# A factorization machine on one core: the first half's input loads go in pairs

## What is computed

```python
x_reg = input_data @ W_lin.T + b_lin
emb = input_data @ factors
sum_squared = jnp.square(emb.sum(axis=1))
squared_sum = (jnp.square(input_data) @ jnp.square(factors)).sum(axis=1)
h = jax.nn.relu(emb @ W1.T + b1)
h = jax.nn.relu(h @ W2.T + b2)
dnn_out = h @ W3.T + b3
x = x_reg + 0.5 * (sum_squared - squared_sum)[:, None] + dnn_out
x = 0.5 + jax.nn.sigmoid(x) * 5.0
```

## Time and profile before

| | us |
|---|---|
| median of 3 runs | 135.52 |
| lowest, highest | 135.15, 135.66 |
| the profiled execution | 135.22 |
| its span, first to last instruction | 133.0 |
| TensorE busy | 104.9 (79%) |
| VectorE busy | 53.3 (40%) |
| ScalarE busy | 64.1 (48%) |
| DMA, mean over the span | 393 GB/s |

### The profile page before, as it was taken

How to read it: one execution, slowest core, us unless ns; L and a number is a source line. 1 busy time by engine, 2 the same in 40 slices (tenths; PEclk the granted TensorE clock), 3 DMA queues, 4 the chain that set the end, 5 groups by cost and what they waited for, 6 DMA issues and landing times.

```text
span 133.0 us, 2839 instructions
## 1 busy us (share of the span) xinstructions
PE 104.9 (79%) x1113; PEld 31.9 (24%) x1113; DVE 53.3 (40%) x51; ACT 64.1 (48%) x72; POOL 13.7 (10%) x48
## 2 busy tenths in 40 slices
PE   6088976939978778877878869996966966989992
PEld 6022211102211111111212312211111111345871
DVE  0391550423522531531540291550451451576571
ACT  4030752625724733733744294752652662465851
POOL 3017011010410110011011001152000000000000
PEclk9999999995999999999999999999999999999999
DMA  4999999999999999999999999999999999999700
GB/s 121 404 398 424 424 438 419 434 414 434 429 429 429 424 434 419 434 429 429 429 434 424 424 429 424 434 429 429 414 438 419 428 442 418 401 416 411 296 14 1
DMA packets 4592, 52.25 MB, mean 393 GB/s; under 512 B 530, under 2 KB 662, under 8 KB 1642
## 3 DMA queue, kind: packets, MB, share of 16 engines
q1 hardware_dynamic: 4586, 52.16, 93.4%
HBM read 52.16 MB, written 0.00 MB: 392 GB/s over the span
## 4 chain that ended last, share of the span: by engine, by line
DMA 62%; PE 29%; ACT 3%; SPq 3%; issue 2%; DVE 1%; ACTq 0%
DMA xr<-in_x_groups 51%; PE p_lin L460 23%; DMA xr<-in_x_end 11%; ACT sq L292 2%; PE p_sq L460 2%; PE p_h L543 2%; SPq L230 1%; PE p_tot L460 1%; PE p_h L574 1%; PE p_tot L556 0%; DVE h L412 0%; DVE h L407 0%; SPq L228 0%; SPq L227 0%; PE p_tot L563 0%
## 5 line engine op out<-in xcount | busy, mean ns | idle before, releaser
L292 ACT ACTIVATE sq<-xr 128x1536 f32<-128x1536 f32 (+1 forms) x40 | 48.5, 1262 | 47.7 <-DMA xr<-in_x_groups 47.7
L387 DVE TENSOR_TENSOR sq<-xr 128x1536 f32<-128x1536 f32 x20 | 35.1, 1759 | 57.0 <-DMA xr<-in_x_groups 56.9
L460 PE MATMUL p_lin<-xr,wr 128*17 128x512 f32 x320 | 38.9, 604 | 16.0 <-DMA xr<-in_x_groups 16.0
L460 PE MATMUL p_lin<-sq,wz 128*18 128x512 f32 x320 | 39.3, 608 | 2.3 <-ACT sq L292 1.0
L460 PEld LDWEIGHTS p_lin<-xr,wr 128*17 128x17 f32 x320 | 8.0, 97 | 45.0 <-issue 24.4
L460 PEld LDWEIGHTS p_lin<-sq,wz 128*18 128x18 f32 x320 | 8.4, 99 | 33.0 <-ACT sq L292 18.7
L267 POOL COPY wr<-hd x20 | 8.4, 422 | 70.9 <-PE p_lin L460 70.4
L395 DVE TENSOR_TENSOR sq<-xr 128x320 f32<-128x320 f32 (+5 forms) x15 | 10.4, 724 | 8.1 <-DMA xr<-in_x_end 8.1
L301 ACT ACTIVATE sq<-xr 128x320 f32<-128x320 f32 (+5 forms) x15 | 9.1, 652 | 7.1 <-DMA xr<-in_x_end 7.1
L460 PE MATMUL p_lin<-xr,hd 128*17 128x352 f32 (+1 forms) x128 | 10.0, 380 | 1.5 <-DMA xr<-in_x_end 1.5
L460 PE MATMUL p_lin<-sq,ws 128*18 128x352 f32 x64 | 6.6, 459 | 0.0
(11 more groups left out here) (50 smaller groups left out, 35.7 us busy)
## 6 DMA issues: line engine op xcount, KB each, us to landing
xr<-in_x_groups SPq DMA_DIRECT2D x20, 2048.0 KB, 15.4
xr<-in_x_end SPq DMA_DIRECT2D x1, 2112.0 KB, 10.8
xr<-in_x_end SPq DMA_DIRECT2D x3, 640.0 KB, 12.3
xr<-in_x_end SPq DMA_DIRECT2D x1, 1760.0 KB, 14.6
xr<-in_x_end SPq DMA_DIRECT2D x1, 1056.0 KB, 12.6
hd<-in_head SPq DMA_DIRECT2D x1, 935.0 KB, 4.8
xr<-in_x_end SPq DMA_DIRECT2D x1, 704.0 KB, 14.0
xf<-in_x_first SPq DMA_DIRECT2D x1, 512.0 KB, 5.8
```

Of the source, the lines that this page charges most:

```text
L292: nc.scalar.activation(sq[:, s, c:c + n, :], xr[:, s, c:c + n, :], ACT.Square).then_inc(act_squared, 1)
L387: nc.vector.tensor_tensor(sq[:, s, 0:BY_DVE, :], xr[:, s, 0:BY_DVE, :], xr[:, s, 0:BY_DVE, :], ALU.mult).then_inc(dve_squared, 1)
L460: return nc.tensor.matmul(out, lhsT, rhs, start=False, stop=False, skip_group_check=True)
```

## The change

The host puts groups 0 and 1, 2 and 3, and so on of the first half side by side, so that one partition's row of a pair is 32 KB of memory without a gap (`x_pairs`). One DMA brings such a pair into two neighbouring slots and counts on the even slot's semaphore. The first half so has 6 DMAs of 4 MB in place of 12 of 2 MB. The second half and `x_end` keep their sizes.

In the first half TensorE multiplies both groups of a pair and then adds the squares of both. The first squares' matmul of each group, issued when the group is multiplied and all of its squares are made, increments a new semaphore, `x_used`; SP waits for that one in the first half, for both groups of a pair, and no longer for `sq_used`. From the first group of the second half on, SP waits for `sq_used` as it did.

TensorE in the first half's loop before: two groups, one after the other. Rows named `xr,wr` multiply, rows named `sq,wz` add squares.

The diff's core:

```diff
+TWO = 2
+PAIR_PITCH = TWO * CHUNKS * HALF + 64
...
+        def landed(engine, r, s, h):
+            if h == 0:
+                engine.wait_ge(x_landed[s - s % TWO], 16 * (r + 1))
+            elif s % TWO == 0:
+                engine.wait_ge(x_landed[s], 16 * (r + 1))
+            else:
+                engine.wait_ge(x_landed[s], 16 * (r + (1 - ROUNDS[0])))
...
-            for s in range(RING):
-                sp.dma_start(xr[:, s].rearrange("p c b -> p (c b)"), x_groups[s, :, 0:CHUNKS * HALF]).then_inc(x_landed[s], 16)
+            for t in range(RING // TWO):
+                sp.dma_start(xr[:, TWO * t:TWO * t + TWO].rearrange("p s c b -> p (s c b)"),
+                             x_pairs[t, :, 0:TWO * CHUNKS * HALF]).then_inc(x_landed[TWO * t], 16)
-            with sp.Fori(1, sum(ROUNDS)) as r:
+            with sp.Fori(1, ROUNDS[0]) as r:
+                for t in range(RING // TWO):
+                    sp.wait_ge(x_used, RING * r + (TWO * t + TWO - RING))
+                    sp.dma_start(xr[:, TWO * t:TWO * t + TWO].rearrange("p s c b -> p (s c b)"),
+                                 x_pairs[bass.ds(RING // TWO * r + t, 1), :, 0:TWO * CHUNKS * HALF]
+                                 .rearrange("g p n -> (g p) n")).then_inc(x_landed[TWO * t], 16)
+            with sp.Fori(ROUNDS[0], sum(ROUNDS)) as r:
...
-                pe.wait_ge(act_squared, len(BY_ACT) * g + 1)
+                pe.wait_ge(act_squared, len(BY_ACT) * g + (2 if h == 0 else 1))
                 for c in range(BY_DVE + BY_ACT[0]):
-                    add_mm(quad(p_lin[h], c, WZ, 0, HALF), wz[:, s, c, :], sq[:, s, c, :])
-                pe.wait_ge(act_squared, len(BY_ACT) * g + 2)
+                    mm = add_mm(quad(p_lin[h], c, WZ, 0, HALF), wz[:, s, c, :], sq[:, s, c, :])
+                    if h == 0 and c == 0:
+                        mm.then_inc(x_used, 1)
+                if h == 1:
+                    pe.wait_ge(act_squared, len(BY_ACT) * g + 2)
...
             with pe.Fori(0, ROUNDS[0]) as r:
-                for s in range(RING):
-                    multiply(r, s, 0)
-                    add_squares(r, s, 0)
+                for t in range(0, RING, TWO):
+                    for s in range(t, t + TWO):
+                        multiply(r, s, 0)
+                    for s in range(t, t + TWO):
+                        add_squares(r, s, 0)
```

More of the change, by code:

```diff
@@ L33 @@
 W_END = ALL - ENDS
-assert GROUPS % RING == 0 and (ALL - 1) % CHUNKS == 0 and END_GROUPS == RING
+assert RING % TWO == 0 and GROUPS % RING == 0 and (ALL - 1) % CHUNKS == 0 and END_GROUPS == RING
 BY_DVE = 3
@@ L73, with fm_kernel @@
 HD = HD_L + LIN
-def fm_kernel(nc, head, x_first, x_rest, x_groups, x_end, out):
+def fm_kernel(nc, head, x_first, x_rest, x_pairs, x_groups, x_end, out):
     with ExitStack() as ctx:
@@ L140, in fm_kernel @@
         dve_squared = sem("dve_squared")
+        x_used = sem("x_used")
         sq_used = sem("sq_used")
@@ L236, in _ @@
                     sp.dma_start(xr[:, s].rearrange("p c b -> p (c b)"),
-                                 x_groups[bass.ds(RING * r + s, 1), :, 0:CHUNKS * HALF].rearrange("g p n -> (g p) n")
-                                 ).then_inc(x_landed[s], 16)
+                                 x_groups[bass.ds(RING * r + (s - GROUPS), 1), :, 0:CHUNKS * HALF]
+                                 .rearrange("g p n -> (g p) n")).then_inc(x_landed[s], 16)
             at = 0
@@ L284, in _, with squares @@
             nc.scalar.activation(sqf[:, :], xf[:, :], ACT.Square).then_inc(first_squared, 1)
-            def squares(r, s):
-                act.wait_ge(x_landed[s], 16 * (r + 1))
+            def squares(r, s, h):
+                landed(act, r, s, h)
                 act.wait_ge(sq_used, RING * r + s + 1)
@@ L324, in _ @@
                 for s in range(RING):
-                    squares(r, s)
+                    squares(r, s, 0)
             act.wait_ge(sq_used, RING + GROUPS)
@@ L336, in _ @@
                 for s in range(RING):
-                    squares(r, s)
+                    squares(r, s, 1)
             square_end(0, 0)
@@ L381, in _, with squares @@
             nc.vector.tensor_tensor(sql[0:REST, :], xl[0:REST, :], xl[0:REST, :], ALU.mult).then_inc(rest_squared, 1)
-            def squares(r, s):
-                dve.wait_ge(x_landed[s], 16 * (r + 1))
+            def squares(r, s, h):
+                landed(dve, r, s, h)
                 dve.wait_ge(sq_used, RING * r + s + 1)
@@ L492, in multiply @@
             def multiply(r, s, h):
-                pe.wait_ge(x_landed[s], 16 * (r + 1))
+                landed(pe, r, s, h)
                 pe.wait_ge(wr_ready, RING * r + s + 1)
@@ L668 @@
     chunks = xT[P + REST:].reshape(ALL - 1, P, B)
-    x_groups = np.zeros((TOTAL, P, PITCH), f32)
-    for g in range(TOTAL):
-        h, c = g // GROUPS, CHUNKS * (g % GROUPS)
-        x_groups[g, :, :CHUNKS * HALF] = chunks[c:c + CHUNKS, :, h * HALF:(h + 1) * HALF].transpose(1, 0, 2).reshape(P, -1)
+    x_pairs = np.zeros((GROUPS // TWO, P, PAIR_PITCH), f32)
+    for g in range(GROUPS):
+        at = g % TWO * CHUNKS * HALF
+        x_pairs[g // TWO, :, at:at + CHUNKS * HALF] = \
+            chunks[CHUNKS * g:CHUNKS * (g + 1), :, :HALF].transpose(1, 0, 2).reshape(P, -1)
+    x_groups = np.zeros((TOTAL - GROUPS, P, PITCH), f32)
+    for g in range(TOTAL - GROUPS):
+        x_groups[g, :, :CHUNKS * HALF] = \
+            chunks[CHUNKS * g:CHUNKS * (g + 1), :, HALF:].transpose(1, 0, 2).reshape(P, -1)
     ends = chunks[ALL - 1 - ENDS:]
```

2 lines of the change are left out of this document (1 added, 1 removed).

## The result

| | before | after |
|---|---|---|
| median, us | 135.50 | 140.25 |
| lowest, highest | 135.15, 135.66 | 138.61, 141.53 |
| the profiled execution | 135.22 | 138.61 |
| its span | 133.0 | 136.4 |

The ratio is 1.031, with an interval from 1.022 to 1.041; it is made from means, and one disturbed run (141.53) is left out of it. The changed kernel is slower by 3%, and the forecast of 135.04 us, with its range up to 136.3, was wrong. The profiled execution is the quickest of the four of the changed kernel. The trace explains its 3.4 us. The others took 1.5 us and more beyond it, of which there is no trace.

A forecast was written before the change was run, and what follows sets the result against it. The prediction took the DMA stream up to piece 1's landing, plus a fixed 16.2 us tail, to bound the kernel. Six fewer DMAs save 0.48 us and nothing else costs time: 135.52 - 0.48 = 135.04 us, range 134.4 to 136.3.

The forecast's parts named there:

- What bounds the kernel: Whole kernel: DMA engines never stop until the input is in; time is piece 1's landing, then 16.2 us to the span's end.
- The saving: First-half loads: six fewer DMAs of 128 rows at 0.08 us each save 0.48 us.
- The rival that 32 KB rows save nothing: First-half loads: a 32 KB row goes as two pieces, nothing is saved, 135.5 us; chance 0.10.
- The deadline: First-half pair slots: a pair must be given back within 8.4 us of landing, 9.71 less a lead of 1.3.
- one to one: First-half queue: each microsecond a pair returns later than 8.4 us after landing costs one microsecond.
- The return: First-half pairs: given back some 5.9 us after landing, 7.3 us with one fall of the clock.
- two falls: Dry-queue case: two clock falls in one pair make its return 5.9 + 2.8 = 8.7 us, 0.3 us late.
- The spare of 2.5 us at full clock: First-half pair slots: time left between a pair's return at 5.9 us and the deadline of 8.4 us.
- The half change: Between halves: TensorE 2.7 us late, group 12's slot back at 83.8, needed at 86.2; 2.4 us to spare, no loss.
- The start: First pair lands at 18.1 us in place of 13.2; engines start 4.9 us later and lose nothing.
- The dry queue: Rival at SP's wait on `x_used` or the second half's first wait: queue runs dry, 136.5 us, 135.8 if seldom; chance 0.17.
- The lag rival: One DMA engine's lag, 1.27 us at group 3, changes: gone 133.8 us, chance 0.08; doubled 136.3 us, chance 0.05.

The follow-up runs named there:

- the two six-slot kernels: Changed kernel with six slots of x (three pairs) in the first half, pairs loaded by one 4 MB DMA or by two of 2 MB: 136.56 and 136.49 us.
- the run with the falls mostly removed: Changed kernel plus small matmuls on zeros, ten at TensorE's start and eight before each pair: 138.11 us, ratio 1.020.
- all five six-slot kernels: Changed kernel with six slots: written-out loads 136.56; two DMAs per pair 136.49; looped loads 135.96, then with small matmuls 136.33 or ScalarE squaring in one instruction 136.22 us.

## Why the prediction was wrong, point by point

**What bounds the kernel** held. The time is piece 1's landing and a fixed tail: 16.2 us forecast, 16.1 measured, and the landing's 3.46 us are the span's 3.4.

**The saving** held in kind and nearly in size: 0.08 us per DMA of 128 rows by the forecast, 0.065 by the two six-slot kernels (0.055 to 0.08 with the others), so 0.39 us for six instead of 0.48. It shows as the earlier end of the first half (68.04 and 68.06 against 68.35) wherever the queue stays full. The rival that 32 KB rows save nothing falls with it.

**The deadline** is the step that failed first. The prediction had 9.71 - 1.3 = 8.4 us after a landing. The lead of 1.3 us was about right. Two things were missing. The engines have nothing left to begin well before a landing counts. For the pair of 29.03, fifteen engines ended between 26.4 and 27.5, the sixteenth, held up by a load of instructions at 24.46, at 28.4, and the landing was marked some 0.5 us after that. And a dry queue starts slowly, which the price of "one to one" put at nothing: for the pair of 49.66 the engines stood still for only 0.35 us on average, but their first packets then took 1.9 us instead of 1.22, and the next landing was 1.0 us late. I had taken the landing as the moment at which the queue is empty. The runs put the deadline at some 6.3 us.

**The return** was forecast at 5.9 us and came to 6.4 at full clock. Multiplies and the first squares' block were right (3.44 + 1.72 us of it). The rest, from the second group's first squares to SP's issue, was 35.41 - 32.49 - 1.72 = 1.2 us. The forecast's parts for it are 0.6, 0.2 and 0.2 us; with all three the return is 6.2 us, with the 0.6 alone 5.8, and the 5.9 that was carried on is neither. With a fall it was 8.1 us instead of 7.3, because a fall costs 1.7 us and not 1.4; group 3's 1.4 us held part of a block at full clock. For the first pair the forecast's "two falls" gave 8.7 and 8.9 came, as 6.4 + 2.5 and not 5.9 + 2.8; that they are so near is luck. The spare of 2.5 us at full clock was in truth about none, and every fall was over the edge.

**The half change** failed at the place and not at the size of its numbers. I followed group 12's slot to the load of group 16: forecast back at 83.8 and needed at 86.2; it came at 86.03 and the landing behind it was not late. I didn't follow the load of group 12 itself. It waits for `sq_used`, so for the whole block of squares of group 8 where `x_used` asks for the first of them, and came 67.66 - 60.40 = 7.3 us after pair 4's landing, with a single group's 4.9 us to bring and the next issue only at 69.38. That made group 12 late by 0.7 us. A fall of the clock in pair 4 was part of it: in the run with the falls mostly removed the same load came 64.92 - 59.37 = 5.6 us after the landing, and group 12 wasn't late. The other 1.1 us, at group 14, are an engine set back by a load of instructions. In the kernel before, two such loads, at 78.49 and 93.90, moved no landing by more than 0.1 us: one engine had been 1.3 us behind since group 3, and an engine that falls behind no further than that one delays nothing. The dry queue had let it catch up (at the landing of 70.02 by the engines' reports, the last two are 0.4 us apart), so the next set-back was paid anew. Before, slots came back one by one here, with 14.7 us still in line.

**The start** was right: the first pair landed at 18.27, forecast 18.1, and nothing followed from that.

**The rivals.** The dry queue was the right one, with its place and mechanism named; I gave it 136.5 us and a chance of 0.17. Its price was counted from the wrong deadline, and as only the time by which a pair misses it. By its own steps with 6.3 in place of 8.4, and 6.4 and 8.1 for the returns, every pair with a fall would have been 1.8 us late, and one at full clock on the edge; the forecast would have been on the slower side. The prediction's own test spoke for it: "if a slice's DMA digit fell under 9 in the middle of the first half, if a pair came back later than 8.4 us". The lag rival was right in its cause, a load of instructions, and had a part in the loss: the step was paid a second time, at group 14, for 1.1 us. Its way there, through the dry queue that evened the engines out, wasn't forecast.

**The sum after the fact**, for the profiled execution: 0.29 us won by fewer DMAs (68.35 - 68.06), 2.06 lost to the gaps behind the pairs (70.12 - 68.06), 1.74 from there to group 15 (0.7 of the dry queue, 1.1 of the load of instructions), and 0.05 less in the rest of the second half. That makes 3.46 us, the distance between 116.81 and 120.27. The median lost 1.3 us more than that; the changed kernel's executions spread over 3 us where those of before spread over 0.5, and a queue at its edge would do that, but no trace shows it.

## What to carry to other kernels

A slot count is judged by how far ahead of the landing in front each load is issued: for the pairs of 4 MB here 3.5 us were enough, but for one loss of 0.3 us, and 2.3 were not; a single group of 2 MB still lost 0.9 us at 3.7. Twice the load in the same memory is half the slots, and the 0.065 us that each saved DMA was worth is no price for that. Where one ring gives way to another, follow the first load of the new one as closely as the last of the old, because its wait may be another.

## What the runs showed of the hardware

- **A queue that ran dry** costs more than its standstill: a 2 MB load took 8.35 us from issue to landing, where lead and transfer make 6.2. The engines' first packets of 32 KB took 1.9 us instead of 1.22.
- **A load of instructions sets one DMA engine back, and every landing waits for the slowest.** In a stream that is always full the step of 1.27 us is never won back, and it moves with the program: from group 3 to group 0 when TensorE's program grew at its start. Once the queue has run dry the engines are level again, and the next load is paid anew (1.1 us at group 14 of the changed kernel). The time stayed the same (135.24 us): in both kernels the step was paid once.
- **The clock's falls feed themselves.** A pause of 3.5 us was followed by the lower level and 1.7 us of loss; with three pair slots the same falls cost nothing (136.33 us without them, 135.96 with).
- **The last store** took 2.0 to 2.3 us to be seen by SP in all five six-slot kernels and 1.0 in all others. In those five, its fourth packet starts as a load of instructions ends, 0.3 to 0.6 us behind the other three. The rest of the cause is open.
